# Mamba layer with a mixture of experts on one core: four decay buffers, another issue order of the B and C rows, and activation tables loaded early

## The reference

```python
x_ssm, x_gate = split(x @ in_proj_w.T + in_proj_b, 2)
x_conv = silu(causal_conv(x_ssm, conv_w) + conv_b)      # 4 taps
Bm, Cm = split(x_conv @ bc_w.T + bc_b, 2)               # 16 states
dt = softplus(x_conv @ dt_w.T + dt_b)
A  = -exp(A_log)
def step(h, (xt, dtt, Bt, Ct)):
    h = h * exp(dtt[:, :, None] * A) + dtt[:, :, None] * Bt[:, None, :] * xt[:, :, None]
    y = einsum('bdn,bn->bd', h, Ct) + xt * D
    return h, y
y = scan(step, 0, ...) * silu(x_gate)
z = y @ out_w.T + out_b + x;  z = layernorm(z) * ln_g + ln_b
x = layernorm(x + z)
```

## Time and profile before

| | |
|---|---|
| runs: median (lowest to highest) | 1474.12 us (1471.44 to 1475.02) |
| profiled execution: its time, its span | 1474.04 us, 1472.2 us |
| busy: PE, DVE, ACT, POOL (share of the span) | 81%, 75%, 58%, 53% |
| first scan starts, last scan of sequence 7 starts | 47.68 us, 673.56 us |

### The profile page before, as it was taken

How to read it: one execution, slowest core, us unless ns; L and a number is a source line. 1 busy time by engine, 2 the same in 40 slices (tenths; PEclk the granted TensorE clock), 3 DMA queues, 4 the chain that set the end, 5 groups by cost and what they waited for, 6 DMA issues and landing times. The chain is left out here.

```text
span 1472.2 us, 17914 instructions
## 1 busy us (share of the span) xinstructions
PE 1198.7 (81%) x5074; PEld 801.4 (54%) x5074; DVE 1098.6 (75%) x1659; ACT 857.1 (58%) x1354; POOL 778.2 (53%) x519
## 2 busy tenths in 40 slices
PE   7778787887959687666139999999999999999950
PEld 3323243333424243323138888888888888888850
DVE  2889898989888898995427777777777777777743
ACT  3664646565654746431127677677767777776744
POOL 0356556777867686876632444444444444444452
PEclk8899789898968898886559999999999999999985
DMA  1443333544444443432464566556556565555537
GB/s 67 191 149 134 115 130 124 173 158 151 141 154 137 139 163 131 149 117 82 175 227 144 152 155 161 147 156 159 155 148 155 158 156 155 158 157 149 156 42 231
DMA packets 69254, 217.13 MB, mean 147 GB/s; under 512 B 7520, under 2 KB 43232, under 8 KB 56288
## 3 DMA queue, kind: packets, MB, share of 16 engines
q1 hardware_dynamic: 29664, 167.42, 31.6%
q0 software_dynamic: 26880, 36.72, 14.7%
q10 hardware_dynamic: 12672, 12.58, 2.6%
HBM read 165.54 MB, written 51.15 MB: 147 GB/s over the span
## 5 line engine op out<-in xcount | busy, mean ns | idle before, releaser
L511 PE MATMUL p_y<-read,small 128*128 128x512 f32 x512 | 297.3, 714 | 126.8 <-POOL read L1006 126.8
L850 DVE TENSOR_TENSOR_SCAN state<-decay,p_bu 128x1024 f32<-128x1024 f32 x128 | 292.3, 2283 | 33.6 <-ACT decay L677 27.9
L1432 POOL DMA_INDIRECT total<-o_v,tok x144 | 266.5, 1851 | 45.1 <-issue 44.8
L677 ACT ACTIVATE decay<-dt,scan_rate 128x511 f32<-128x511 f32 x256 | 169.2, 712 | 176.2 <-DVE state L850 175.9
L511 PEld LDWEIGHTS p_y<-read,small 128*128 128x128 f32 x512 | 104.9, 220 | 293.0 <-POOL read L1006 193.8
L1430 POOL TENSOR_TENSOR scrap<-neg_half 128x1 f32<-128x1 f32 x36 | 14.6, 405 | 356.3 <-ACT o_v L1317 353.8
L1006 POOL TENSOR_TENSOR read<-state,bc 128x1024 f32<-128x1024 f32 x64 | 150.5, 2351 | 52.4 <-DVE p_bu L841 20.3
L1294 ACT ACTIVATE gate_v<-p_g,bias 128x512 f32<-128x512 f32 x144 | 98.2, 682 | 97.1 <-PE p_up L1243 96.9
L1304 ACT ACTIVATE ah<-a_v 128x512 fp32r<-128x512 f32 x144 | 91.2, 633 | 91.7 <-DVE a_v L1378 91.7
L1006 POOL TENSOR_TENSOR read<-state,first_wh 128x1024 f32<-128x1024 f32 x32 | 75.4, 2355 | 109.7 <-DVE p_bu L841 87.8
L1367 DVE TENSOR_SCALAR up_v<-up_v 128x512 f32<-128x512 f32 x144 | 61.9, 430 | 63.7 <-ACT up_v L1297 63.6
(11 more groups left out here) (209 smaller groups left out, 3007.9 us busy)
## 6 DMA issues: line engine op xcount, KB each, us to landing
bc<-bc_rows SPq DMA_DIRECT2D x32, 1024.0 KB, 5.1
first_raw<-in_w_experts SPq DMA_DIRECT2D x19, 1668.0 KB, 6.7
raw_w<-in_w_experts SPq DMA_DIRECT2D x18, 1668.0 KB, 6.8
first_wh<-bc_rows SPq DMA_DIRECT2D x16, 1024.0 KB, 5.2
first_wl<-bc_rows SPq DMA_DIRECT2D x16, 1024.0 KB, 5.0
first_rows<-queues SPq DMA_DIRECT2D x19, 544.0 KB, 6.8
xq<-queues SPq DMA_DIRECT2D x18, 544.0 KB, 6.9
queues<-read SPq DMA_DIRECT2D x9, 544.0 KB, 4.0
```

Of the source, the lines that this page charges most:

```text
L511: mm = pe.matmul(p_y[h][:, :], ident[:, :], read[:, t % 4, h, :], start=False, stop=(t == SLOTS - 1))
L677: act.activation(decay[t % 2][:, h, 1:LEN], dt[s.p][:, h, 1:LEN], ACT.Exp, scale=rate[:, h, t:t + 1])\
L850: dve.tensor_tensor_scan(flat(state[t % 4][:, :, :]), flat(decay[t % 2][:, :, :]), p_bu[:, :], 0.0, ALU.mult, ALU.add).then_inc(s_state, 1)
L1432: pool.indirect_dma_start(total, bass.IndirectOffsetOnAxis(ap=tok[t.p][:, a:a + 1], axis=0), o_v[t.p][:, a, :], None, compute_op=ALU.add). ...
```

## The change

1. Four decay buffers (AHEAD = 4). ACT issues a state's decay two slots ahead of its scan instead of one, and waits for the scan four states back instead of two. The decays of states 0 and 1 of the next sequence are issued in slots 14 and 15.
2. PE computes dt0 and dt1 ahead of bc, and ACT stores them in this order.
3. SP issues pairs 0 and 1 of a round ahead of the next sequence's xt, in every round that has a scan.
4. In round -1 three tiny activations on a 128x1 tile load tables: SiLU ahead of the first data, Exp after the SiLU of slot 6, Exp after the softplus of slot 9. The gate's SiLU of sequence 0 moves from round -1, slot 14, to round 0, slot 2.
5. The load of x on ACT waits for one more residual (s_residual), and the setup's semaphore counts shift.

```diff
@@ Round.blocks
-                + ["bc", "dt0", "dt1", "in2", "in3"] * a)
+                + ["dt0", "dt1", "bc", "in2", "in3"] * a)
@@ buffers
+    table = sb("table", 1, at=one)
-    RING = 4
+    RING, AHEAD = 4, 4
-    decay = [sb(f"decay{i}", 2, LEN, at=one) for i in range(2)]
+    decay = [sb(f"decay{i}", 2, LEN, at=one) for i in range(AHEAD)]
@@ PE, slot 8
-                    from_xc(r, "bc", BC, 2 * STATE)
                     for i in range(HALVES):
                         from_xc(r, f"dt{i}", DT_ + i * P, P)
+                    from_xc(r, "bc", BC, 2 * STATE)
@@ act_stage1
+        def load_table(func):
+            act.activation(table[:, :], table[:, :], func).then_inc(s_table, 1)
+        act.wait_ge(s_set_dve, 1)
+        load_table(ACT.Silu)
         act.wait_ge(s_first, FIRST_SETUP)
...
         def decays(s, t):
-            after(act, s_state, SLOTS * s.n + t - 1)
+            after(act, s_state, SLOTS * s.n + t - AHEAD + 1)
             if t == 0:
                 act.wait_ge(s_dt, s.n + 1)
             for h in range(HALVES):
-                act.activation(decay[t % 2][:, h, 1:LEN], dt[s.p][:, h, 1:LEN], ACT.Exp, scale=rate[:, h, t:t + 1])\
+                act.activation(decay[t % AHEAD][:, h, 1:LEN], dt[s.p][:, h, 1:LEN], ACT.Exp, scale=rate[:, h, t:t + 1])\
                    .then_inc(s_decay, 1)
...
                 if r.a and t == 6:
                     store_conv(r, 1)
                     silu(r)
+                    if r.like == Round.FIRST:
+                        act.wait_ge(s_table, 1)
+                        load_table(ACT.Exp)
                 if r.a and t == 9:
                     softplus(r)
+                    if r.like == Round.FIRST:
+                        act.wait_ge(s_table, 2)
+                        load_table(ACT.Exp)
...
-                if r.a and t == 14:
+                if r.a and t == 14 and r.b:
                     silu_gate(r)
-                if r.b and t < SLOTS - 1:
-                    decays(r.s, t + 1)
+                if r.like == 0 and t == 2:
+                    silu_gate(Round(r.s.at(-1), Round.FIRST))
                 if r.like == Round.FIRST and t == SLOTS - 1:
                     act.wait_ge(s_set_dve, SET_DVE)
-                if r.next_b and t == SLOTS - 1:
-                    decays(r.s.at(1), 0)
+                    for i in range(AHEAD - 2):
+                        decays(r.s.at(1), i)
+                if r.b and t < SLOTS - AHEAD + 2:
+                    decays(r.s, t + AHEAD - 2)
+                if r.next_b and r.b and t >= SLOTS - AHEAD + 2:
+                    decays(r.s.at(1), t - SLOTS + AHEAD - 2)
...
                 if r.a and t == 8:
-                    store_bc(r)
                     store_dt(r, 0)
                     store_dt(r, 1)
+                    store_bc(r)
@@ sp_stage1
-            if r.a:
+            if r.like == Round.FIRST:
                 load_sequence(r)
-            if r.like == Round.FIRST:
...
             for pair in range(PAIRS):
                 if r.b:
                     replicate(r.s, pair)
+                if r.a and r.b and pair == 1:
+                    load_sequence(r)
```

More of the change, by code:

```diff
@@ L288, in build @@
     s_route, s_rexp, s_chosen, s_index = (sem(n) for n in ("s_route", "s_rexp", "s_chosen", "s_index"))
+    s_table = sem("s_table")
     s_scrap = sem("s_scrap")
@@ L483, in convolve @@
             if r.like == Round.FIRST:
-                pe.wait_ge(s_set_dve, 1)
+                pe.wait_ge(s_set_dve, 2)
             if 0 in some:
@@ L497, in from_xc @@
             bank, done = block(r, name)
-            if name == "bc":
+            if name == "dt0":
                 pe.wait_ge(s_silu, 2 * r.s.at(1).n + 1)
@@ L666, in store_bc @@
             if r.like == Round.FIRST:
-                act.wait_ge(s_set_dve, 2)
+                act.wait_ge(s_set_dve, 3)
             act.activation(bc_out[0:2 * STATE, :], bank[0:2 * STATE, :], ACT.Identity, bias=b_bc2[0:2 * STATE, 0:1])\
@@ L682, in load_x @@
             s = r.s
-            after(act, s_residual, s.n - 1)
+            after(act, s_residual, s.n)
             act.dma_start(x[:, :, :], ins["x"][bass.ds(s.n, 1), :, :].rearrange("s (t p) d -> (s p) t d", p=P))\
@@ L760, in act_stage1 @@
                     start_total(r)
-    SET_DVE = 4
+    SET_DVE = 6
     def dve_setup(dve):
+        dve.memset(table[:, :], 0.0).then_inc(s_set_dve, 1)
         dve.wait_ge(s_first, FIRST_SETUP)
@@ L798, in dve_setup_rest @@
         last.then_inc(s_set_dve, 1)
-        for h in range(2):
-            dve.memset(decay[h][:, :, 0:1], 0.0)
+        for i in range(AHEAD):
+            last = dve.memset(decay[i][:, :, 0:1], 0.0)
+        last.then_inc(s_set_dve, 1)
     def negate_rate(dve):
@@ L849, in scan @@
             after(dve, s_read, n - 3)
-            dve.tensor_tensor_scan(flat(state[t % 4][:, :, :]), flat(decay[t % 2][:, :, :]), p_bu[:, :],
+            dve.tensor_tensor_scan(flat(state[t % 4][:, :, :]), flat(decay[t % AHEAD][:, :, :]), p_bu[:, :],
                                    0.0, ALU.mult, ALU.add).then_inc(s_state, 1)
```

## The result

The changed kernel takes 1450.8 us (median of four runs, 1449.85 to 1455.42) against 1474.26 for the kernel before (four runs, 1471.44 to 1475.02): ratio 0.9852, 95% interval 0.9837 to 0.9868. It is faster by 23.5 us; forecast were 31.6 and 1442.4, so the median lies 8.4 us above the forecast, beyond its own range (up to 1447) and inside the wide one (up to 1452). The profiled execution is the longest of the four: 1455.42, span 1453.6, that is 18.6 shorter than the span of the profiled one before. After the last scan both have the same left to do (798.9 and 798.6 us), so in these two executions all of the difference arises in stage 1.

What follows compares the result with a forecast made beforehand. DVE was taken to set stage 1's pace, waiting mainly for decays, plus a late start. Decay waits 24.7 and start 6.9 sum to 31.6: 1474.0 - 31.6 = 1442.4 us; own range 1438.5 to 1447, wide range 1438 to 1452.

Steps and rivals of the forecast that it cites:

- The waits for the decay: Stage 1, scan 10 of rounds 0 to 6 and scan 7 of round 1: DVE's waits for decay go, 24.7 us gained.
- The 0.2: Short wait before each scan in the hardware loop, put down to the loop's form; expected to stay.
- The 1.09 of scan 7 in round 1: DVE's wait for the decay at that scan, 1.09 us, counted among the eight waits to be removed.
- What is late next is nothing of ACT's, then; DVE's own work.: After scan 10: decay of 11 ready 1.0 ahead, scaled z 0.5 ahead in round 1, so no new wait takes the gain.
- The start: Before the first scan: earlier table loads and first pair gain 6.9 us, between 5.5 (products slow) and 8.3 (full clock).
- The clock's part: PE's twelve products at the start: 2.85 us more gained if they run at full instead of half clock.
- A: Slots 11 and 12: the wait moves instead of going, 2 us back in each of seven rounds, 1456; chance 0.10.
- B: The start gains nothing, as the first pair's rows may land late (up to 12.8); 1449.3; chance 0.11.
- C: PE, left at 1.2 GHz early in its gapless stretch from slot 1, becomes the bound; slower, 1498; chance 0.03.
- D: The scans wait for something other than the decay, so only the start is gained; 1467; chance 0.02.

Runs made afterwards that it cites:

- scale_late: The changed kernel with POOL's scaling of z moved from slot 10 to slot 11, behind the wait for DVE's softplus sum; 1445.27 us.
- psum_operand: The changed kernel with the first softplus instruction on DVE reading p_u from PSUM instead of expo from SBUF, softplus correction left out; 1445.3 us, one run.
- read_late: The changed kernel with POOL's scaling behind slot 11's softplus-sum wait, two scatters moved from slot 10 to 11 and 12, read of state 10 to slot 12; 1432.87 us.
- four_only: The kernel before with only the four decay buffers, decays two slots ahead and the stricter wait of the x load; 1462.26 us.
- scale_twice: The changed kernel with POOL's scaling of z done twice in a row; 1462.77 us, one run.
- bc_first: The changed kernel with bc ahead of dt0 and dt1 again, in PE's products and ACT's stores; 1455.15 us, one profiled run.

## Why the prediction came out as it did

*The waits for the decay (24.7).* Right in place and size: scan 10 of rounds 0 to 6 gave 23.4, and no wait came at scan 11. The 0.2 stayed. The 1.09 of scan 7 in round 1 is also gone, but in the profiled execution PE's product for z held DVE 1.28 in the same slot; in scale_late it did not.

*"What is late next is nothing of ACT's, then; DVE's own work."* This step failed. I asked only whether the next instructions would have to *wait*: the decay of 11, the scaled z, the softplus. None waits (that slack was as worked out). But POOL's chain did not move up with DVE: read 8, the norm's power, two scatters and read 9 end at 309.26 in round 3, then the scaling. Counted from the start of scan 9, the scaling ended 10.48 later before (316.34 to 326.82) and ends 10.36 later now (300.86 to 311.22), and scan 11 starts after 12.62 and 12.51. Before, DVE stood idle for 2.64 of this chain, and the softplus pair came when POOL was nearly through. Now the first of the pair begins inside read 9 and is let in only when the scaling too has ended. A stall of 2.64 on the semaphore became 2.53 inside an instruction. The excess of the softplus pair and the residual over their shortest durations, all rounds, is 3.7 before and 17.9 after, 14.2 given back; the removal experiments show it (psum_operand, read_late).

The trace had it: before the change the line-814 instruction took 1.22 in round 0 and 1.50 to 1.56 in rounds 1 to 6, each time beside the scaling and ending 1.07 to 1.09 after it, and the last residual took 3.02 beside a read. A duration above an instruction's shortest is a wait that no list of waits contains. The Trainium skill says it outright, "SBUF — State Buffer" (SBUF: two separate sides): the pair of ports that the two engines share is a lock for a whole instruction, taken by a GpSimd instruction or by a VectorE one with two SBUF inputs. The runs here agree (4.09, 2.13 and 3.02 beside POOL, 1.21 alone or with a PSUM input). By it the sum would have been worked so: POOL's scaling begins when read 9 has ended, whatever DVE does, and slot 11 returns what slot 10 gained as long as POOL's chain stands.

The kernel's own code had it too. In while_scanning, POOL's read in slot 11 waits for DVE's softplus sum (s_sum), in slot 12 for the residual (s_residual), in slots 13 and 15 for dt and p_u, although it reads none of these. One such wait, in round 3 of the changed kernel:

```profile
313.52 2.34 POOL L1026 TENSOR_TENSOR read<-state,first_wl 128x1024 f32<-128x1024 f32 x1 [2.31 <-DVE first_raw L837]
```

What these waits do is keep POOL's reads away from DVE's instructions with two inputs in SBUF. Read 9 and the scaling stand ahead of the first of them; scale_late puts the scaling behind it.

*The start (6.9, ends 5.5 and 8.3).* Measured from the twelve products, 24.83 - 17.77 = 7.06, and 1.28 for the load ahead of them: 8.3, the upper end, in this pair of executions; the raw difference is 7.7, as the first data came later. The mechanism was right. The clock's part is 2.87 only where the execution before had half clock, as two of four with that gap did. And without the new order of issues neither clock nor table helps: four_only, at full clock, waits 5.36 for its rows.

*Rivals.* A had the right place, slots 11 and 12, and the size (14 given back; its 1456 against this execution's 1455.42 is luck, as the median is 1450.8), but the wrong mechanism: nothing waits there, and it is strongest in rounds 2 to 6 rather than in round 1. B, C and D are out, and that 1450.8 lies near B's 1449.3 is a coincidence: no wait for rows, a round of 80.3 at a clock of 0.85, and 23.4 gained at the scans that were named.

*The sum.* 31.6 + 0.8 (start) - 14.2 (given back) - 1.3 (scan 10 instead of 24.7 in all) + 2.2 (PE's waits and the remainder) = 19.1; the last scan came 18.8 earlier, the span 18.6 shorter. The median is 4.6 below the profiled execution. DVE's waits for PE differ by some of that between executions (round 1 slot 7 and round 2 slot 4 together 3.0 in the changed kernel's and none in scale_late's), and what follows the last scan took 795.3 to 800.6 in the fourteen profiles (798.9 here), but there is no trace of the other three, so this last part is argued, not shown.

## What to carry to other kernels

When a stall on one engine is removed, look at what the other engines did during it: if two of them share something that no semaphore guards, the stall may have been what kept them apart. Compare each instruction's duration with its shortest of the same shape; what is above it is a hidden wait if it ends a fixed time after another engine's instruction; here that was so between VectorE, mostly with both inputs in SBUF, and GpSimd. A semaphore wait that guards no data may be there for this reason. Starting GpSimd's work later, behind the instruction that it would stop, can be the gain: here three moves of POOL's work to later slots brought 18 us (1450.8 to 1432.9; 16.9 of the 23.1 between the two profiles are standstills that went), beside 23.5 for the whole change.

## What the runs showed of the hardware

- A VectorE instruction with two SBUF inputs of 128x1024 (1.22 alone) that begins inside a GpSimd tensor_tensor of the same size ends 1.07 to 1.11 after that ends, in all 120 places of the fourteen profiles where it takes over 1.30. Beside a read and a scaling that follow each other without a gap it stands through both (4.06 to 4.09); wherever the second began 0.07 or more after the first's end (scale_twice, and rounds 3 and 5 of bc_first, among others) it got in between.
- The reverse too: GpSimd's scaling of 2.00 took 2.53 to 3.06 where VectorE's instruction had the start.
- A scan and the product p_bu, each with one input in PSUM, keep 2.29 and 1.23 beside the same instructions.
- One input in SBUF does not make an instruction free of it: VectorE's tensor_scalar of 128x4, in SBUF alone, took 0.52 to 2.12 instead of 0.17 beside a GpSimd read in twelve places of the kernels before and after, and ended 0.02 to 0.04 after it. The batch-norm aggregation just ahead of it kept its 0.18.
- After a gap of 3.08 in PE's work the next twelve products ran at half clock in two executions of four, after 1.80 in none of ten.
